# Two attention layers: scores from two fp16 parts in the array's row halves, in two-bank slots

## The chip, the cores and the metric

The kernel runs on one core of one Trainium2 chip. The metric is the device time of one execution in microseconds (us); lower is better. Engines are named as in the profile: PE (TensorE matmuls; PEld its weight loads), DVE (VectorE), ACT (ScalarE), POOL (GpSimd) and SP (SyncE, which here issues DMAs).

## The reference

A stack of four attention layers and four expert layers on x of 8 batches x 512 tokens x 256 features, fp32. The change touches the third layer ("rope") and the seventh ("latent"). Both compute, cut to what matters:

```python
q, k, v = heads(...)                      # 16 heads of 16 features each
q = q * cos + rotate_half(q) * sin        # rotary embedding, the same for k
scores = einsum('bqhd,bkhd->bhqk', q, k) * DH ** -0.5
attn = softmax(scores, axis=-1)           # 512 x 512 for each of 8 batches x 16 heads
out = einsum('bhqk,bkhd->bqhd', attn, v)
x = x + out.reshape(b, l, d) @ Wo         # latent adds a bias; its q is x itself
```

In rope q, k and v are projections of the normalised x. In latent q is the normalised x and k and v come through 128-wide latents, whose two matrices are folded into one before. The layer "decay" before rope has the same shape and keeps the old code.

## The kernel before

Everything is written out by hand for each engine: each has one list of instructions in program order, and semaphores tie the lists together. The layers run one after the other. `mha_layer` builds decay, rope and latent.

**The scores.** A score must be accurate to fp32, and the fast matmul takes bf16. So each rotated q and k is split into three bf16 parts. Of the products of parts six are kept; with 16 features a head that makes 96 rows of contraction. The rows stand in `QS` and `KS` in SBUF, written through DRAM (`write_parts`, L1435; `load_group`, L1448). Softmax needs the row maximum before the exponential. So the scores are computed twice: `max_scores` (L1553) with queries on the partitions, for DVE's maximum over 512 keys (`maxima`, L1819), and `exp_scores` (L1566) with keys on the partitions, for ACT's exponential (L1733), where three more rows (96 to 98) subtract the maximum, itself in three bf16 parts. `split_maxima` (L1839 to L1846) makes these parts, PE turns them (`mT`, L1526), ACT copies them and one DMA writes them into `QS` (L1456).

**The loop.** A batch has 64 steps, one for each of 16 heads x 4 key tiles. In a step PE issues one exp score matmul and one max score matmul of 512 columns, ACT one exponential and DVE one maximum of 128x512. The maxima run 13 to 28 steps ahead. Max scores have three PSUM banks (`psA`) and exp scores two (`psB`), apart from each other. After every fourth step PE multiplies the four probabilities tiles by the values (`value_sums`, L1597: fp32, four heads in four column quarters of the array, two instructions each). The table `USES` puts the rest of PE's work, called uses, into given steps: transposes of the normalised x (`xT`), the projections (`k`, `q`, `v`), the turned outputs (`OT`, `aT`) and the output projection (`Wo`). They share two PSUM banks (`psM`) in turn. ACT empties most of them; DVE normalises the heads from OT (L1853, L1855) and adds Wo to x, with the next layer's statistics (L1868 to L1876).

**The preparation of the next batch.** DVE normalises x (L1774, L1779), shuffles for the rotation (L1805) and multiplies with the cosines (L1793). POOL multiplies with the sines (L1381), adds (L1383), makes part one (L1392) and the two differences (L1396, L1402); ACT makes part two (L1694). Per batch these are four such chains (k and q, each in two halves of 8 heads). SP then writes the parts to DRAM and loads them back. `QS` and `KS` hold one batch, in four groups of four heads.

**The lead-in.** The first batch's chains run on DVE and ACT alone. DVE also adds the expert layer's results of batches 4 to 7 in between (L407, L410, L413). No exponential starts before the first group's maxima are in `QS`.

## Time and profile before

| what | value |
|---|---|
| time, median of 3 runs | 2992.68 us (2987.15 to 2997.36) |
| profiled execution, first to last instruction | 2991.6 us |
| PE / DVE / ACT / POOL busy | 83% / 68% / 54% / 28% |
| mean granted PE clock | 0.915 |
| rope, first to last exponential | 959.6 to 1485.3 us |
| latent, first to last exponential | 2199.5 to 2704.9 us |

The profiled execution's own time is given only as its span, 2991.6 us, 1.1 us below the median of the runs. The shares are averages over layers with different limits, so the two layers are read in windows of their own. A duration of a PE row holds the time until its result is out. The issue of matmuls that follow each other is read from the difference of their starts.

### The profile page before, as it was taken

How to read it: one execution, taken by the hardware profiler on the slowest of the kernel's cores; microseconds unless marked ns; L12 is line 12 of the kernel's file. 1: busy time of each engine (PE TensorE's matmuls, PEld its weight loads, DVE VectorE, ACT ScalarE, POOL GpSimd, SP SyncE). 2: the span in 40 equal slices, each digit the busy share in tenths (PEclk: the TensorE clock that was granted, in tenths of full speed). 3: DMA queues.
4: the chain of work that ended last, by engine and by line, in shares of the span. 5: the costliest groups of instructions: out<-in, count | busy, mean ns of one | idle time of the engine just before them, and what ended most of it. 6: DMA issues, size and time to landing. Idle time of an engine off the chain costs nothing. (4 is left out here: it accounts for less than half of the span.)

```text
span 2991.6 us, 42513 instructions
## 1 busy us (share of the span) xinstructions
PE 2494.0 (83%) x13800; PEld 1260.0 (42%) x13800; DVE 2037.1 (68%) x5246; ACT 1603.7 (54%) x3058; POOL 848.9 (28%) x777
## 2 busy tenths in 40 slices
PE   4899999997575999999857687399789999995598
PEld 2344444443452333333345455266423333333365
DVE  5788888884638788888553444677488888874343
ACT  2477776776423766666652433255347677673122
POOL 0333222220232433322023300445233334302211
PEclk7799999999787999999978899599879999997799
DMA  7565655651164333333026200456343222313232
GB/s 242 179 187 177 181 179 170 179 171 49 56 195 138 96 96 96 101 103 96 13 90 187 66 1 36 175 190 230 124 139 103 90 92 86 116 56 132 96 132 84
DMA packets 217234, 368.47 MB, mean 123 GB/s; under 512 B 21801, under 2 KB 173100, under 8 KB 212280
## 3 DMA queue, kind: packets, MB, share of 16 engines
q1 hardware_dynamic: 201480, 316.35, 33.2%
...
## 5 line engine op out<-in xcount | busy, mean ns | idle before, releaser
L1816 DVE CUSTOM_DVE_ANT_0 decay_junk<-decay_scores_q,decay_corr 128x512 bf16<-128x512 f32 x512 | 338.4, 685 | 111.4 <-PE decay_scores_q L1553 109.6
L1733 ACT ACTIVATE decay_probs<-decay_scores_k 128x512 f32<-128x512 f32 x512 | 294.5, 597 | 188.8 <-PE decay_scores_k L1572 155.1
L1819 DVE TENSOR_REDUCE rope_mx<-rope_scores_q 128x1 f32<-128x512 f32 x512 | 334.0, 685 | 89.9 <-PE rope_scores_q L1553 89.6
L1733 ACT ACTIVATE rope_probs<-rope_scores_k 128x512 f32<-128x512 f32 x512 | 294.6, 600 | 166.3 <-PE rope_scores_k L1566 165.0
L1819 DVE TENSOR_REDUCE latent_mx<-latent_scores_q 128x1 f32<-128x512 f32 x512 | 330.4, 684 | 70.2 <-PE latent_scores_q L1553 69.8
L1733 ACT ACTIVATE latent_probs<-latent_scores_k 128x512 f32<-128x512 f32 x512 | 294.9, 600 | 151.6 <-PE latent_scores_k L1566 149.8
L1553 PE MATMUL decay_scores_q<-decay_KS,decay_QS 96*128 96x512 bf16 x512 | 204.6, 400 | 36.7 <-DVE decay_mx L1816 23.3
L1553 PE MATMUL latent_scores_q<-latent_KS,latent_QS 96*128 96x512 bf16 x512 | 201.3, 395 | 22.7 <-DMA latent_QS<-latent_parts_dram 13.4
L1553 PE MATMUL rope_scores_q<-rope_KS,rope_QS 96*128 96x512 bf16 x512 | 200.8, 394 | 21.5 <-DVE rope_mx L1819 12.8
L1566 PE MATMUL latent_scores_k<-latent_QS,latent_KS 99*128 99x512 bf16 x512 | 197.3, 387 | 6.0 <-ACT latent_probs L1733 2.8
L1566 PE MATMUL rope_scores_k<-rope_QS,rope_KS 99*128 99x512 bf16 x512 | 196.7, 386 | 4.5 <-ACT rope_probs L1733 2.7
L1569 PE MATMUL decay_scores_k<-decay_QS,decay_KS 99*128 99x384 bf16 (+3 forms) x512 | 156.6, 307 | 15.0 <-DMA decay_QS<-decay_mT 7.2
L1597 PE MATMUL decay_out_heads<-decay_probs,decay_Vaug 128*32 128x512 f32 x1024 | 139.0, 615 | 0.8 <-DVE decay_probs L1828 0.8
L1597 PE MATMUL rope_out_heads<-rope_probs,rope_Vaug 128*32 128x512 f32 x1024 | 136.4, 605 | 0.7 <-ACT rope_probs L1733 0.7
L1597 PE MATMUL latent_out_heads<-latent_probs,latent_Vaug 128*32 128x512 f32 x1024 | 136.4, 605 | 0.7 <-ACT latent_probs L1733 0.7
L208 PE MATMUL experts_logits_results<-experts_we,experts_xT 128*128 x384 | 114.2, 426 | 14.4 <-ACT experts_xT L262 9.7
L1566 PEld LDWEIGHTS latent_scores_k<-latent_QS,latent_KS 99*128 99x128 bf16 x512 | 49.1, 97 | 182.6 <-ACT latent_probs L1733 138.3
L1566 PEld LDWEIGHTS rope_scores_k<-rope_QS,rope_KS 99*128 99x128 bf16 x512 | 49.0, 96 | 181.8 <-ACT rope_probs L1733 149.2
L1569 PEld LDWEIGHTS decay_scores_k<-decay_QS,decay_KS 99*128 99x128 bf16 x512 | 49.4, 97 | 174.9 <-issue 86.0
L1381 POOL TENSOR_TENSOR rope_sh<-rope_sh,rope_tab 128x512 f32<-128x512 f32 x28 | 35.5, 1268 | 304.3 <-DVE rope_fc L1793 304.3
L348 DVE TENSOR_TENSOR experts_y<-experts_logits_results,experts_be 128x256 f32<-128x256 f32 x96 | 39.6, 424 | 104.8 <-PE experts_logits_results L208 72.6
L765 ACT ACTIVATE experts4x_hT<-experts4x_inner 128x512 f16<-128x512 f32 x64 | 38.2, 597 | 125.6 <-PE experts4x_inner L669 125.6
...
## 6 DMA issues: line engine op xcount, KB each, us to landing
decay_KS<-decay_parts_dram SPq DMA_DIRECT2D x64, 384.0 KB
decay_QS<-decay_parts_dram SPq DMA_DIRECT2D x64, 384.0 KB
decay_parts_dram<-decay_parts SPq DMA_DIRECT2D x56, 384.0 KB, 3.1
...
```

The source lines that it names most:

```text
L208: last = pe.matmul(psL[:, n % 2, 0:D], xT[:, n % 2, c, :], we[:, c, bass.ds(at, D)], start=(c == 0), stop=(c == 1))
L348: dve.tensor_tensor(y[:, n % RING, :], psL[:, n % 2, 0:D], be[:, bass.ds(at, D)], ALU.add).then_inc(y_taken, 1)
L765: act.activation(hT[:, 0, f, :], psH[:, (n * FC + f) % 3, :], ACT.Relu).then_inc(h_high, 1)
L1381: eng.tensor_tensor(sh[:, j % 2, :], sh[:, j % 2, :], tab[:, 1, :], ALU.mult).then_inc(sin_done, 1)
L1553: pe.matmul(psA[:, A_BANK[k], :], QS[0:96, 0, c, hh, qt * P:(qt + 1) * P], KS[0:96, NV - 1, c, hh, :], start=True, stop=True).then_inc(a_r ...
L1566: last = pe.matmul(psB[:, s % 2, :], KS[:, 0, c, hh, keys], QS[:, 0, c, hh, :], start=True, stop=True)
L1569: last = pe.matmul(psB[:, s % 2, 0:end], KS[:, 1, c, hh, keys], QS[:, 0, c, hh, 0:end], start=True, stop=True)
L1597: last = pe.matmul(psO[32 * h:32 * h + 32, :], Vaug[:, b % 2, kt, 4 * grp + h, :], probs[:, (b * 16 + kk) % PSLOTS, h, :], start=(kt == 0) ...
L1733: act.activation(probs[:, (b * 16 + kk) % PSLOTS, h, :], psB[:, s % 2, :], ACT.Exp, scale=scale).then_inc(exp_done, 1)
L1816: dve.tensor_tensor_reduce(junk[:, a % 2, :], psA[:, A_BANK[k], :], corr[:, qt, :], 1.0, -3.0e38, ALU.mult, ALU.max, mx[:, grp % 2, qt, h: ...
L1819: dve.tensor_reduce(mx[:, grp % 2, qt, h:h + 1], psA[:, A_BANK[k], :], AX.X, ALU.max).then_inc(a_done, 1)
```

## The change

Rope and latent are built by a new function, `mha_pairs`. Decay keeps `mha_layer`.

- Each rotated q and k is split into two fp16 parts. Three of their products are kept: 48 rows of contraction for a head. To stay in fp16's range, k and q are scaled by powers of two that are found once in the lead-in from the largest weight (`scales`); in latent the tables hold a factor of 32.
- Two heads are handled in a step. One stands in partitions 0 to 47, the other in 64 to 111, so each matmul uses one half of the array's rows. The two results go into the two banks of one slot. Two more rows in each half (48 and 49) subtract the maximum in two fp16 parts.
- A batch has 32 steps. In each, PE issues two exp score matmuls and two max score matmuls, ACT one exponential and DVE one maximum, each of 128x1024.
- PSUM: max and exp scores share one ring of three two-bank slots, taken in turn. The uses share one bank in place of two.
- The maxima run 16 steps ahead. Their parts are turned by DVE (32x32 blocks), written to DRAM and read back by SP into `QS`.
- `QS` and `KS` hold two batches, each in two halves of 8 heads.
- POOL takes over the cosine products (L1793 before) and the normalising of x after the first two batches (L1774, L1779 before). The middle part on ACT and one difference go.
- `value_sums` is as before, after every second step. `USES` is a new table, with a use in every even step (rope) or all but two of these (latent).

The core of the diff:

```diff
+def mha_pairs(nc, g, ins, project_q, biased, results):
...
+    STEPS, NM = 32, 8
...
+    USES = [(0, "k0"), (2, "q0"), (4, "OT3"), (6, "aT1"), (8, "Wo0"), (10, "Wo1"), (12, "OT0"), (14, "k1"), (16, "q1"),
+            (18, "v0"), (20, "OT1"), (22, "aT0"), (24, "v1"), (26, "xT0"), (28, "OT2"), (30, "xT1")]
+    if not project_q:
+        USES = [(u, name) for u, name in USES if name[0] != "q"]
...
+    ROTATE_AT = [2, 4, 16, 18]
+    NORMALISE_AT, PV_AT = 18, 1
...
+    scores = [("top", n) for n in range(16)]
+    for n in range(NB * STEPS):
+        scores += [("exp", n)] + ([("top", n + 16)] if n + 16 < NB * STEPS else [])
...
+        psS = ctx.enter_context(nc.psum_tensor(f"{g['layer']}_scores", [P, 3, 2, S], F32))
+        psO = ctx.enter_context(nc.psum_tensor(f"{g['layer']}_out_heads", [P, S], F32))
+        psM = ctx.enter_context(nc.psum_tensor(f"{g['layer']}_work", [P, S], F32))
...
+        parts = sb("parts", [P, 4, 2, S], F16)
+        QS, KS = (sb(n, [P, 2, 2, 4, S], F16) for n in ("QS", "KS"))
+        probs = sb("probs", [P, 2, 4, S], F32)
...
+        def wait_slot(eng, kind, n):
+
+            at = place[kind, n] - 3
+            if at >= 0:
+                before, k = scores[at]
+                eng.wait_ge(exp_done if before == "exp" else a_done, k + 1)
...
+            def write_parts(nb, j):
+
+                o, c = CHAINS[j]
+                sp.wait_ge(low_done, nb * 4 + j + 1)
+                rows = rows_of(nb, o, c).rearrange("(j d) (h t) -> (d h) j t", d=16, h=8)
+                for first, n, i in ((0, 2, 0), (2, 1, 1)) if o == "k" else ((1, 2, 0), (0, 1, 1)):
+                    sp.dma_start(rows[:, first:first + n, :], parts[:, j, i:i + 1, :].to_broadcast([P, n, S])).then_inc(
+                        parts_written[j], 16)
+
+            def load_half(nb, c):
+
+                for j in (2 * c, 2 * c + 1):
+                    sp.wait_ge(parts_written[j], 32 * (nb + 1))
+                if nb >= 2:
+                    sp.wait_ge(b_ready, (nb - 2) * STEPS + 16 * (c + 1))
+                for o, to in (("k", KS), ("q", QS)):
+                    for y in range(2):
+                        sp.dma_start(to[64 * y:64 * y + 48, nb % 2, c, :, :].rearrange("r l s -> r (l s)"),
+                                     rows_of(nb, o, c)[:, 4 * y * S:(4 * y + 4) * S]).then_inc(half_loaded[c], 16)
...
+                             mpT[:, n % 2, :]).then_inc(rows_written[n % 2], 16)
+
...
+                sp.wait_ge(rows_written[n % 2], 16 * (n // 2 + 1))
+                for y in range(2):
+                    sp.dma_start(QS[64 * y + 48:64 * y + 50, nb % 2, c, at:at + 2, :],
+                                 rowscr[n][4 * y:4 * y + 4, :]).then_inc(rows_loaded[grp], 16)
...
+            def max_scores(n):
...
+                wait_slot(pe, "top", n)
+                qt, hp = divmod(a, 2)
+                c, l = heads_of(grp, hp)
+                for y in range(2):
+                    rows = slice(64 * y, 64 * y + 48)
+                    last = pe.matmul(psS[:, slot_of("top", n), y, :], QS[rows, nb % 2, c, l, qt * P:(qt + 1) * P],
+                                     KS[rows, nb % 2, c, l, :], start=True, stop=True)
+                last.then_inc(a_ready, 1)
...
+            def exp_scores(b, u):
...
+                wait_slot(pe, "exp", b * STEPS + u)
+                c, l = heads_of(grp, hp)
+                for y in range(2):
+                    rows = slice(64 * y, 64 * y + 50)
+                    last = pe.matmul(psS[:, slot_of("exp", b * STEPS + u), y, :],
+                                     KS[rows, b % 2, c, l, kt * P:(kt + 1) * P], QS[rows, b % 2, c, l, :], start=True, stop=True)
+                last.then_inc(b_ready, 1)
...
+                pe.wait_ge(exp_done, b * STEPS + 2 * kk + 2)
...
+            for b in range(NB):
+                for u in range(STEPS):
+                    exp_scores(b, u)
+                    if top_of(b, u) is not None:
+                        max_scores(top_of(b, u))
+                    if u % 2 == PV_AT:
+                        if u > PV_AT:
+                            value_sums(b, u // 2 - 1)
+                        elif b:
+                            value_sums(b - 1, 15)
+                    for name, nb in uses_at(b, u):
+                        work(name, nb)
...
+                    if u % 2 == 0 and kk >= 2:
+                        act.wait_ge(pv_done, kk - 1)
+                    act.wait_ge(b_ready, n + 1)
+                    act.activation(probs[:, kk % 2, 2 * (u % 2):2 * (u % 2) + 2, :], psS[:, slot_of("exp", n), :, :], ACT.Exp,
+                                   scale=escale[:, 0:1]).then_inc(exp_done, 1)
+                    if u % 8 == PV_AT + 1:
+                        if grp:
+                            take_heads(b, grp - 1)
+                        elif b:
+                            take_heads(b - 1, 3)
+                    for name, nb in uses_at(b, u - 1) if u else uses_at(b - 1, STEPS - 1):
+                        if name[:2] not in TURNED_BY_DVE:
+                            take(name, nb)
...
+            def rotate(nb, j):
+
+                n = nb * 4 + j
+                of, src = turned_from(j)
+                emptied(dve, of, nb)
+                if n >= 2:
+                    dve.wait_ge(sum_done, n - 1)
+                dve.stream_shuffle(sh[:, j % 2, :], src, [i ^ 8 for i in range(32)]).then_inc(rot_done, 1)
...
+            def maxima(n):
...
+                dve.wait_ge(a_ready, n + 1)
...
+                dve.tensor_reduce(mx[:, grp % 2, :, hp, qt], psS[:, slot_of("top", n), :, :], AX.X, ALU.max).then_inc(a_done, 1)
...
+                flat = mx[:, grp % 2, :, :, :].rearrange("p y l t -> p y (l t)")
+                dve.tensor_scalar(mp[:, 0, :, 0, :], flat, -1.0 / LEVEL, None, ALU.mult).then_inc(split_done, 1)
+                dve.wait_ge(split_done, 2 * n + 1)
+                dve.scalar_tensor_tensor(mp[:, 0, :, 1, :], flat, -1.0 / LEVEL, mp[:, 0, :, 0, :], ALU.mult,
+                                         ALU.subtract).then_inc(split_done, 1)
...
+                dve.transpose(mpT[:, n % 2, :], mp[:, 0, :, :, :].rearrange("p y s r -> p (y s r)")).then_inc(rows_turned, 1)
...
+            for b in range(NB):
+                for u in range(STEPS):
+                    if top_of(b, u) is not None:
+                        maxima(top_of(b, u))
+                    if u % 8 == 0 and b * 4 + u // 8 + 1 < NB * 4:
+                        split_maxima(*divmod(b * 4 + u // 8 + 1, 4))
+                    for name, nb in uses_at(b, u - 1) if u else uses_at(b - 1, STEPS - 1):
+                        if name[:2] in TURNED_BY_DVE:
+                            (normalise_heads if name[:2] == "OT" else add_out)(nb, int(name[-1]))
+                    if b + 1 < NB and u in ROTATE_AT:
+                        rotate(b + 1, ROTATE_AT.index(u))
...
+            for b in range(NB):
+                for u in range(STEPS):
+                    if b + 2 < NB and u == NORMALISE_AT:
+                        pool.wait_ge(m_ready, turn["xT1", b + 1] + 1)
+                        for t in range(4):
+                            normalise(pool, b + 2, t)
+                        if biased:
+                            add_bias(b + 2)
+                    if b + 1 < NB and u in ROTATE_AT:
+                        j = ROTATE_AT.index(u)
+                        cosines(pool, b + 1, j)
+                        rotary_sum(pool, b + 1, j)
+                        high_part(pool, b + 1, j)
+                        low_part(pool, b + 1, j)
+
+
 def single_head_layer(nc, g, ins, results):
...
-                "rope", mha_layer, rope, False, HD ** -0.5, True, False, (), results))
+                "rope", mha_pairs, rope, True, False, results))
...
-                "latent", mha_layer, latent, False, HD ** -0.5, False, True, (), results))
+                "latent", mha_pairs, latent, False, True, results))
```

TensorE's order, a stretch of a middle batch of rope, before:

```order
L1566 MATMUL rope_scores_k<-rope_QS,rope_KS 128x512
L1553 MATMUL rope_scores_q<-rope_KS,rope_QS 128x512
L1597 MATMUL rope_out_heads<-rope_probs,rope_Vaug 32x512 x4
L1566 MATMUL rope_scores_k<-rope_QS,rope_KS 128x512
L1553 MATMUL rope_scores_q<-rope_KS,rope_QS 128x512
L1566 MATMUL rope_scores_k<-rope_QS,rope_KS 128x512
L1553 MATMUL rope_scores_q<-rope_KS,rope_QS 128x512
L1526 MATMUL rope_work<-identb,rope_mp 12x128 x4
L1566 MATMUL rope_scores_k<-rope_QS,rope_KS 128x512
L1553 MATMUL rope_scores_q<-rope_KS,rope_QS 128x512
L1539 MATMUL rope_work<-rope_wo,rope_attnT 128x256 x2
```

The same engine in a middle batch of the changed rope (L2305 exp scores, L2292 max scores, L2318 values, L2278 and L2261 uses):

```order
L2305 MATMUL rope_scores<-rope_QS,rope_KS 128x512 x2
L2292 MATMUL rope_scores<-rope_KS,rope_QS 128x512 x2
L2318 MATMUL rope_out_heads<-rope_probs,rope_Vaug 32x512 x4
L2305 MATMUL rope_scores<-rope_QS,rope_KS 128x512 x2
L2292 MATMUL rope_scores<-rope_KS,rope_QS 128x512 x2
L2278 MATMUL rope_work<-rope_wv,rope_xnT 128x256 x4
L2305 MATMUL rope_scores<-rope_QS,rope_KS 128x512 x2
L2292 MATMUL rope_scores<-rope_KS,rope_QS 128x512 x2
L2318 MATMUL rope_out_heads<-rope_probs,rope_Vaug 32x512 x4
L2305 MATMUL rope_scores<-rope_QS,rope_KS 128x512 x2
L2292 MATMUL rope_scores<-rope_KS,rope_QS 128x512 x2
L2261 MATMUL rope_work<-ident_sb,rope_xn 128x128 x4
```

Between two values there are now two pairs of each kind where there were four single matmuls of each. The uses come as a whole after a pair of pairs, where a large one was cut in halves before. The turning of the maxima (L1526) is gone.

SP's order for one middle batch of rope, before, from the row maxima of group 1 to those of the next batch's group 0:

```order
L1456 DMA rope_QS<-rope_mT 3x4x512
L1435 DMA rope_parts_dram<-rope_parts 128x3x512
L1435 DMA rope_parts_dram<-rope_parts 128x2x512
L1435 DMA rope_parts_dram<-rope_parts 128x512
L1435 DMA rope_parts_dram<-rope_parts 128x3x512
L1435 DMA rope_parts_dram<-rope_parts 128x2x512
L1435 DMA rope_parts_dram<-rope_parts 128x512
L1456 DMA rope_QS<-rope_mT 3x4x512
L1448 DMA rope_KS<-rope_parts_dram 96x2048
L1448 DMA rope_QS<-rope_parts_dram 96x2048
```

And the changed one, from the row maxima of group 3 (L2210 writes them to DRAM, L2219 reads them) to those of the next batch's group 0, with the parts of chains 2 and 3 (L2192) and the load of the second half (L2203):

```order
L2210 DMA rope_tops_dram<-rope_mpT 4x32x32
L2219 DMA rope_QS<-rope_tops_dram 2x1024 x2
L2192 DMA rope_parts_dram<-rope_parts 128x2x512
L2192 DMA rope_parts_dram<-rope_parts 128x512
L2192 DMA rope_parts_dram<-rope_parts 128x2x512
L2192 DMA rope_parts_dram<-rope_parts 128x512
L2210 DMA rope_tops_dram<-rope_mpT 4x32x32
L2203 DMA rope_KS<-rope_parts_dram 48x2048 x2
L2203 DMA rope_QS<-rope_parts_dram 48x2048 x2
L2219 DMA rope_QS<-rope_tops_dram 2x1024 x2
```

A row maximum takes two transfers where it took one. The next batch's first maxima are read after the load of its second half, which waits for the parts of chains 2 and 3.

VectorE's order in a middle batch of the changed rope, around the two additions to x (L2503 maxima, L2537 to L2545 the addition and its statistics, L2524 and L2526 the normalising of heads):

```order
L2503 TENSOR_REDUCE rope_mx<-rope_scores 128x2
L2537 TENSOR_TENSOR X<-X,rope_work 128x2x256
L2540 BN_STATS rope_st<-X 128x6 x2
L2543 BN_AGGR rope_mv<-rope_st 128x2 x2
L2545 COPY X<-rope_mv 128x2x2
L2503 TENSOR_REDUCE rope_mx<-rope_scores 128x2 x2
L2537 TENSOR_TENSOR X<-X,rope_work 128x2x256
L2540 BN_STATS rope_st<-X 128x6 x2
L2543 BN_AGGR rope_mv<-rope_st 128x2 x2
L2545 COPY X<-rope_mv 128x2x2
L2503 TENSOR_REDUCE rope_mx<-rope_scores 128x2 x2
L2524 RECIPROCAL rope_rec<-rope_work 128x16
```

One maximum now covers what two did, so the two additions stand two maxima apart; before it was also two, of half the size.

## Rows read from the trace of the kernel before

**Rows 1.** Busy time of rope's lead-in, rope's middle and latent's middle:
```profile
core 0: us, PE busy (x) PEld busy (x) DVE busy (x) ACT busy (x) POOL busy (x), PEclk, DMA share, GB/s
902.40:959.60 57.20, 32.03 (x74) 11.80 (x75) 49.07 (x120) 15.42 (x32) 16.33 (x16) 0.65 0.56 172
...
1052.00:1446.00 394.00, 386.29 (x2043) 149.19 (x2042) 321.27 (x671) 268.63 (x497) 123.29 (x110) 1.00 0.30 94
...
2265.00:2651.00 386.00, 376.65 (x2042) 145.90 (x2041) 329.90 (x709) 270.73 (x499) 145.84 (x125) 1.00 0.31 98
```

**Rows 2.** Rope's and latent's exponentials, all of the run:
```profile
L1733 ACT ACTIVATE rope_probs<-rope_scores_k x512: 582/597/631, 959.6 to 1485.3; 128x512 f32<-128x512 f32 x171
...
L1733 ACT ACTIVATE latent_probs<-latent_scores_k x512: 582/597/629, 2199.5 to 2704.9; 128x512 f32<-128x512 f32 x171
```

**Rows 3.** Groups by line (busy, mean ns, idle before), middles of rope, latent:
```profile
L1566 PE MATMUL rope_scores_k<-rope_QS,rope_KS 99*128 99x512 bf16 x376 | 144.6, 385 | 1.5 <-ACT rope_probs L1733 0.4
...
L1819 DVE TENSOR_REDUCE rope_mx<-rope_scores_q 128x1 f32<-128x512 f32 x378 | 247.7, 685 | 68.3 <-PE rope_scores_q L1553 68.2
...
L1566 PE MATMUL latent_scores_k<-latent_QS,latent_KS 99*128 99x512 bf16 x381 | 146.6, 385 | 1.6
```

**Rows 4.** TensorE in order of time, one stretch of rope's middle:
```profile
1200.70 0.63 PE L1531 MATMUL rope_work<-ident_sb,rope_Osb 128*128 128x128 f32 x4
1201.16 0.38 PE L1566 MATMUL rope_scores_k<-rope_QS,rope_KS 99*128 99x512 bf16 x1
1201.38 0.38 PE L1553 MATMUL rope_scores_q<-rope_KS,rope_QS 96*128 96x512 bf16 x1
1201.69 1.06 PE L1597 MATMUL rope_out_heads<-rope_probs,rope_Vaug 128*32 128x512 f32 x8
1202.69 0.39 PE L1566 MATMUL rope_scores_k<-rope_QS,rope_KS 99*128 99x512 bf16 x1
...
1204.43 1.03 PE L1539 MATMUL rope_work<-rope_wo,rope_attnT 128*128 128x256 f32 x4
1205.30 0.38 PE L1566 MATMUL rope_scores_k<-rope_QS,rope_KS 99*128 99x512 bf16 x1
```

**Rows 5.** Groups by shape in the causal layer:
```profile
L2164 ACT ACTIVATE causal_probs<-causal_masked,causal_nm 128x512 f32<-128x512 f32 x8 | 5.8, 722 | 25.1 <-DVE causal_nm L2242 25.1
...
L2239 DVE CUSTOM_DVE_ANT_0 causal_masked<-causal_scores,causal_mask 128x512 f32<-128x512 f32 x8 | 5.5, 692 | 22.1 <-PE causal_scores L2071 22.1
...
L2164 ACT ACTIVATE causal_probs<-causal_masked,causal_nm 128x128 f32<-128x128 f32 x8 | 3.2, 402 | 2.7 <-DVE causal_nm L2242 2.7
...
L2239 DVE CUSTOM_DVE_ANT_0 causal_masked<-causal_scores,causal_mask 128x128 f32<-128x128 f32 x8 | 2.3, 292 | 37.1 <-PE causal_scores L2071 21.7 <-DMA rope_KS<-rope_onesrow 15.3
```

**Rows 6.** VectorE groups beside the maxima, rope's middle; latent's normalising:
```profile
L1793 DVE TENSOR_TENSOR rope_fc<-rope_f,rope_tab 128x512 f32<-128x512 f32 x21 | 15.6, 742 | 0.0
L1805 DVE STREAM_SHUFFLE rope_sh<-rope_f 128x512 f32<-128x512 f32 x21 | 15.5, 736 | 0.0
...
L1774 DVE TENSOR_SCALAR rope_xn<-X 128x256 f32<-128x256 f32 x20 | 8.1, 405 | 0.0
...
L1779 DVE TENSOR_SCALAR latent_xn<-X 128x128 f32<-128x128 f32 x40 | 12.9, 389 | 0.0
```

**Rows 7.** VectorE in order of time, end of rope:
```profile
1493.22 0.69 DVE L1868 TENSOR_TENSOR X<-X,rope_work 128x512 f32<-128x512 f32 x1 [4.03 <-PE rope_work L1539]
...
1495.09 0.68 DVE L1868 TENSOR_TENSOR X<-X,rope_work 128x512 f32<-128x512 f32 x1
```

**Rows 8.** GpSimd groups, rope's middle:
```profile
L1383 POOL TENSOR_TENSOR rope_fc<-rope_fc,rope_sh 128x512 f32<-128x512 f32 x22 | 28.1, 1277 | 1.7
...
L1392 POOL CAST rope_parts<-rope_fc 128x512 bf16<-128x512 f32 x22 | 15.5, 704 | 1.4
```

**Rows 9.** DMA issues (KB each, median us to landing):
```profile
rope_parts_dram<-rope_parts SPq DMA_DIRECT2D x32, 384.0 KB, 2.7
rope_KS<-rope_parts_dram SPq DMA_DIRECT2D x32, 384.0 KB, 4.1
```

424 lines of the change are left out of this document (418 added, 6 removed).

## The prediction

> **What bounds the kernel now.** I read the busy windows first, to see which engine is full in the two changed layers, then the groups by line, then TensorE in order of time. In rope's middle, 394 us, PE is busy 386 at a granted clock of 1.00, DVE 321 and ACT 269; latent's middle looks alike [rows 1]. Those 394 us hold 376 exponentials, so a batch of 64 takes 67.1 us; latent's 381 in 386 us give 64.8 [rows 1, 3]. Exp scores waited 1.5 us in all and the maxima 68 us, nearly all for PE [rows 3]. So PE sets the pace and DVE is next.
>
> PE's time is in the starts, not the durations. A score matmul issues every 0.22 us (1201.16 to 1201.38). A values group costs 0.31 from the score before it, and 1.00 to the score after it: 1.31, or 1.09 more than a score alone. A turned OT costs 0.46 and half a Wo 0.87 [rows 4]; a k or q projection streams as many columns as a whole Wo (1.73). Before, a rope batch needs 128 x 0.22 = 28.2, 16 x 1.09 = 17.4, eight large uses 13.8, eight small ones 3.9, and four turned maxima 1.6 (at 0.4 each, less than an OT): 64.9 of the 67.1. In latent, without q, 61.5 of the 64.8.
>
> **The scores on PE.** If the two row halves run side by side, a pair of 512 columns costs the 0.22 of one: 64 x 0.22 = 14.1, so 14.1 go. No row here has row halves. The nearest are the values: eight instructions of 512 columns in four column quarters issue in 1.00 us, where eight in a row at a score's pace would need 1.76 [rows 4]. The array does run quarters side by side. The bounds are 0.22 and 0.44 a pair; I take 0.22.
>
> A score after values waits longer than a score after a score: entering costs 0.09 more, and leaving about 0.15 (1.00 against the 0.85 of a half Wo's columns) [rows 4]. The switch to and from a use costs nothing visible today. The changed scores stand in a layout of the array that neither values nor uses have, so I charge 0.24 for each of 16 uses: 3.9 us; none and 0.48 are the bounds. The four turned maxima (1.6) go. PE then needs 14.1 + 17.4 + 13.8 + 3.9 + 3.9 = 53.1 us for a rope batch and 49.2 for latent.
>
> The Trainium skill, "TensorEngine Tiling (Array Packing)", Tiling Modes, says that a change of tiling mode drains the engine. That speaks against this change, which has more of them; the trace agrees at the values, with the 0.09 and 0.15 above. With no drain charged at the uses the PE sum would be 49.2 for rope.
>
> **DVE and ACT.** The slopes come from the causal layer: DVE 692 to 292 ns over 384 columns is 1.04 ns a column, ACT 722 to 402 is 0.83 [rows 5]. A maximum of 1024 then takes 685 + 533 = 1.22 us, 1.18 back to back, so 32 of them 37.9 us where 64 take 42.2 [rows 3]. An exponential takes 0.60 + 0.43 = 1.03: 33 us a batch, with 14 copies of some 0.58 (estimate from the 0.60) 41. ACT stays third.
>
> DVE's other work is (321.3 - 247.7) / 5.87 batches = 12.5 us [rows 1, 3]. The cosine products (four of 0.74) and rope's normalising (four of 0.41) leave it [rows 6]; with one operation less in the split and a transpose more, about 9 of work and 11 to 12 with the waits between dependent operations remain. DVE needs some 49 us, close to PE's 53.
>
> **What the shared slots make of it.** PE's and DVE's sums aren't reached, because buffering gets thinner. An exp pair may be written only when the maximum of two steps before is done, a max pair only when the exponential of the step before is done. So PE can run about one step ahead of DVE, where it had separate rings before. I count by pairs of steps, each the larger of two sums:
> - PE: an odd step is 0.44 + 1.09 = 1.53, an even step with a large use 0.44 + 1.97 = 2.41, with a small one about 1.17. So 3.94 or 2.70 (2.8 with the waits for the shared bank).
> - DVE: 2.36 for two maxima, and beside them a shuffle 0.62, a split 0.6, a normalising of heads 0.7, or an addition to x with its statistics, 1.87 [rows 7].
> - Rope: six pairs with a large use at 3.94; the two with Wo are DVE's, 4.9 and 4.3; the pair at step 4 3.7; three with heads 3.1; four 2.8. The sum is 23.6 + 9.2 + 3.7 + 9.3 + 11.2 = 57. Waits of uses for their one bank (a k projection behind the normalising of heads, twice) add about 2: 59.
> - Latent: two of the large pairs lose q and become 3.1 and 3.8: 56 to 58.
>
> **The preparation on POOL, and SP.** The chain is now cosine, sine, sum, high, low: 4 x 1.27 + 0.70 = 5.8 us [rows 8]. Its start is a shuffle in steps 2, 4, 16 and 18. POOL also normalises between chains 2 and 3. POOL has no row for this; its sum takes 1.27 where DVE's product takes 0.74, so I scale by 1.8 [rows 6, 8]: rope 4 x 0.73 = 2.9. Latent 8 x 0.70 = 5.6, and 2.4 for the bias. Bounds are DVE's own times (1.6 and 3.1) and twice my figures. In rope step 16 is at about 32 us: shuffle at 34.5, chain 2 to 40.5, normalising to 43.4, chain 3 to 49.2, parts out at 53.3 (1.1 to issue, 2.7 to 3 to land), loads issued to 55, landed at 58.5 (half the size of a 4.1 us load today) [rows 9]. It is needed at 59: just in time. In latent the same gives 61 to 61.5 against 58, so the next batch's first scores wait some 3 us and a batch takes 61.5. That cost has no cover: exp and max scores of step 0 both stand behind it. The row maxima's way through DRAM (about 0.7 + 2.5 + 1.4 + 2.5 = 7 us) lies inside eight steps of 1.8 us, and the scratch traffic falls to half.
>
> **The sum.** Rope: six middle batches 6 x (67.1 - 59) = 49. First and last took 526 - 6 x 67.1 = 124 together [rows 2]. The new first lacks four uses (54), and the new last has maxima only in its first 16 steps and then runs at ACT's pace (46): with a cold start 104, so 20. Rope 69. Latent: 6 x (64.8 - 61.5) = 20, and 117 against 102 for first and last: 15; 35. The lead-ins get longer: the power-of-two scales (some ten small operations across PE and DVE), the second batch normalised and turned ahead of the first maximum, and the first row maxima through DRAM. In rope's lead-in PE has only 0.65 of its clock and is busy 32 of 57 us, so nothing there is PE's [rows 1]. I count 5 for rope and 4 for latent, between 0 (hidden behind the additions of results) and 10 each. Gain 69 + 35 - 9 = 95. From the span of 2991.6, that is 2897; the median of the runs is 1.1 higher, so I say 2897.
>
> **Rivals.**
> - *Free flow.* Uses don't pay for a switch, waits overlap better, and both layers run at 55 and 57: rope 6 x 12.1 + 24 = 97, latent 6 x 7.8 + 20 = 67, less 9: 2837. For it: PE before reached 97% of its sum. Against: slots are coarser and DVE at 49 of 55 would be nearly full.
> - *Late halves.* POOL's normalising or the DMAs are slower than I scale, and each batch ends in a wait: rope 62, latent 66. Rope 31 + 16, latent -7 + 8, less 12: 2956. For it: the time to the deadline in rope is under 1 us. Against: SP and POOL are otherwise free.
> - *Row halves in turn (the slower side).* If a pair costs 0.44, PE needs 67.2 in rope and 63.3 in latent, and with the loss to thin slots 70.5 and 68.5. Middles lose 20 and 22, first and last give back 14, the lead-ins cost 12: 3032. The point where it decides: a pair of about 0.33, where PE's 60 passes DVE's pair sums. For it: each half needs its own weights, and a weight load of 128 columns hides behind 0.22 us today, but two must. Against: the four quarters of the values. The Trainium skill, "TensorE: Matmul & The Clock Gate", Part 3, gives 3.07 times for four row tiles; no run here shows it. By that a pair would cost about 0.25 and the rope batch 2 us more, on PE only.
> - The clock is no case of its own. The middles run at 1.00, which is 2.4 GHz, and the lead-in, where PE waits for long, at a mean of 0.65 [rows 1]. Waits of a microsecond between PE's 53 of 59 us should not bring it down; if a wait of several did, each batch of the late halves would lose a microsecond more, and that case would end at 2970.
>
> **Chances.** Forecast 0.56, free flow 0.14, late halves 0.15, halves in turn 0.15. Within 0.3% (9 us, about what a measurement of this kernel can tell from no change) lies only a thin part between the last two, 0.04. Faster by more 0.84, slower by more 0.12. The forecast's own range is 2865 to 2935; the range of 8 in 10 takes in free flow and late halves, 2835 to 2970, and leaves out halves in turn.
>
> **What would show it.** Rope's exponentials to be 256 of about 1.03 us, maxima 256 of 1.22; the two matmuls of a pair to start within a few tens of ns and the next pair 0.22 later; an issue of 0.3 between scores and a use; middle batches of 59 and 61.5 us; DVE busy about 0.83 of them; in latent a wait of some 3 us for a DMA into KS or QS each 32 steps. I am wrong if the second matmul of a pair starts 0.2 us after the first, if POOL's normalising is over 1 us each, or if DVE and PE wait for each other all along with neither over 0.8.

## The result, and the profile after

| | before | changed kernel |
|---|---|---|
| time, median | 2993.65 us (2987.15 to 2997.36, 4 runs) | 2944.56 us (2938.81 to 2948.00, 4 runs) |
| profiled execution | 2991.6 us | 2937.1 us |
| rope, first to last exponential | 525.7 us | 465.6 us |
| latent, first to last exponential | 505.4 us | 495.5 us |
| middle batches, rope / latent | 68.2 / 65.1 us | 59.5 to 61.5 / 65.3 to 65.9 us |

The ratio is 0.983, interval 0.982 to 0.985: 49 us less, where 95 were forecast. Between the two profiled executions it is 54.5 us, since the changed kernel's is the fastest of its four. Rope gave 60 of the 69 forecast, latent 10 of 35. The lead-ins cost 6.1 and 6.6 us more than before, where 5 and 4 were charged. Together that is 57 us; the 3 between it and the 54.5 lie in stretches that the change leaves alone. These move by several us from execution to execution: rope's start lies anywhere from 896.7 to 904.6 us in the runs below. A middle batch is the time from its first exponential to the next batch's; before, the six rope ones had a first-to-first time of 68.2, a little over the 67.1 that [rows 1, 3] gave by count.

First the busy time by windows, which answers to [rows 1]: rope's lead-in, rope's middle, latent's batches from the second on, and 6 us behind one of latent's borders.

```profile
core 0: us, PE busy (x) PEld busy (x) DVE busy (x) ACT busy (x) POOL busy (x), PEclk, DMA share, GB/s
911.00:968.20 57.20, 30.99 (x76) 12.05 (x76) 44.36 (x98) 15.24 (x31) 11.79 (x12) 0.62 0.30 82
1020.00:1378.00 358.00, 326.65 (x2002) 113.52 (x1998) 292.62 (x431) 250.32 (x274) 156.70 (x140) 1.00 0.20 55
2216.00:2650.00 434.00, 354.13 (x2232) 120.51 (x2228) 321.69 (x477) 282.82 (x300) 177.10 (x165) 0.95 0.17 45
...
2281.00:2287.00 6.00, 6.00 (x26) 1.90 (x26) 2.92 (x5) 2.73 (x3) 0.00 (x0) 0.74 0.02 3
```

In rope PE is busy 0.91 and DVE 0.82. In latent PE has 0.82 and DVE 0.74: both wait for something else. The exponentials and the groups by line of rope's middle, which answer to [rows 2, 3, 6, 8]:

```profile
L2426 ACT ACTIVATE rope_probs<-rope_scores,rope_escale x256: 1106/1114/1172, 968.2 to 1433.8; 128x1024 f32<-128x1024 f32 x128
```
```profile
L2426 ACT ACTIVATE latent_probs<-latent_scores,latent_escale x256: 1107/1115/1172, 2152.9 to 2648.4; 128x1024 f32<-128x1024 f32 x128
```
```profile
L2503 DVE TENSOR_REDUCE rope_mx<-rope_scores 128x2 f32<-128x1024 f32 x191 | 233.2, 1224 | 61.5 <-PE rope_scores L2292 60.8
...
L2305 PE MATMUL rope_scores<-rope_QS,rope_KS 50*128 50x512 f16 x384 | 74.8, 386 | 6.6 <-DMA rope_QS<-rope_tops_dram 5.4 <-DVE rope_mx L2503 1.3
...
L2148 POOL TENSOR_TENSOR rope_parts<-rope_fc,rope_parts 128x512 f16<-128x512 f32 x24 | 27.8, 1157 | 1.9
L2160 POOL TENSOR_SCALAR rope_xn<-X 128x256 f32<-128x256 f32 x20 | 24.2, 1219 | 0.0
```

A maximum took 1.224 us (forecast 1.22), an exponential 1.115 (1.03), one of POOL's normalisings in rope 1.22 (0.73). Next, PE in order of time across a border of two rope batches, in answer to [rows 4]; in a score row x2 is one pair, one matmul in each row half.

```profile
1202.11 0.39 PE L2305 MATMUL rope_scores<-rope_QS,rope_KS 50*128 50x512 f16 x2
1202.34 0.38 PE L2292 MATMUL rope_scores<-rope_KS,rope_QS 48*128 48x512 f16 x2
...
1206.21 0.39 PE L2305 MATMUL rope_scores<-rope_QS,rope_KS 50*128 50x512 f16 x2 [0.89 <-DMA rope_QS<-rope_tops_dram]
1206.44 0.38 PE L2292 MATMUL rope_scores<-rope_KS,rope_QS 48*128 48x512 f16 x2
1206.75 1.98 PE L2265 MATMUL rope_work<-rope_xnT,rope_wk 128*128 128x512 f32 x4
1208.66 0.39 PE L2305 MATMUL rope_scores<-rope_QS,rope_KS 50*128 50x512 f16 x2
```

The pair takes the 0.39 of one matmul and the next pair starts 0.23 later: the row halves run side by side. From scores into a use it takes 0.31 (1206.44 to 1206.75), and at rope's border the row maxima come 0.89 us late (2.2 at the worst border): "just in time", as forecast. Latent's border is another matter. First what PE waited for in latent, then PE, SP and POOL at one border.

```profile
PE latent_scores L2305 <- DMA latent_QS<-latent_tops_dram: 37.4, 6, 6.6
PE latent_scores L2292 <- ACT latent_probs L2426: 19.3, 23, 1.1
PE latent_work L2272 <- DVE latent_attn L2526: 7.7, 14, 0.7
PE latent_work L2265 <- DVE latent_attn L2526: 7.3, 7, 1.1
```
```profile
2273.79 1.06 PE L2318 MATMUL latent_out_heads<-latent_probs,latent_Vaug 128*32 128x512 f32 x8
2280.99 0.61 PE L2305 MATMUL latent_scores<-latent_QS,latent_KS 50*128 50x512 f16 x2 [6.14 <-DMA latent_QS<-latent_tops_dram]
2281.40 0.63 PE L2292 MATMUL latent_scores<-latent_KS,latent_QS 48*128 48x512 f16 x2
2281.96 3.06 PE L2265 MATMUL latent_work<-latent_xnT,latent_wk 128*128 128x512 f32 x4
```
```profile
2273.02 0.52 SPq L2210 DMA_DIRECT2D latent_tops_dram<-latent_mpT  x1
2274.67 0.79 SPq L2203 DMA_DIRECT2D latent_KS<-latent_parts_dram  x2
2275.51 0.89 SPq L2203 DMA_DIRECT2D latent_QS<-latent_parts_dram  x2
2276.44 0.57 SPq L2219 DMA_DIRECT2D latent_QS<-latent_tops_dram  x2
```
```profile
2251.51 1.27 POOL L2127 TENSOR_TENSOR latent_fc<-latent_f,latent_tab 128x512 f32<-128x512 f32 x1 [15.83 <-DVE latent_sh L2495]
...
2257.32 6.51 POOL L2165 TENSOR_SCALAR latent_xn<-X 128x128 f32<-128x128 f32 x8
2263.91 2.37 POOL L2603 TENSOR_TENSOR X<-X,latent_xb 128x1024 f32<-128x1024 f32 x1
2266.24 1.27 POOL L2127 TENSOR_TENSOR latent_fc<-latent_xnT,latent_tab 128x512 f32<-128x512 f32 x1
...
2270.91 1.16 POOL L2148 TENSOR_TENSOR latent_parts<-latent_fc,latent_parts 128x512 f16<-128x512 f32 x1
```

Read backwards: PE stood 6.14 us for the row maxima's DMA, which stood in SP's queue behind the loads of the second half, and these behind chain 3, which stood on POOL behind 8.9 us of normalising and bias. Ahead of it POOL had been idle for 15.83 us. And the wait has a second price: the granted clock behind the border is 0.74 (a mix of 2.4 and 1.2 GHz; PE had been idle for 6 us), so the k projection takes 3.06 us and not 1.98.

### The profile page after: what moved, and what is told of

Same layout as the page of the kernel before. It is cut to its first block and busy times, and to the rows that moved or that the text cites. A ratio compares the mean times of both kernels' runs of the same rounds, so it can differ in the third digit from the quotient of the medians.

```text
span 2937.1 us, 40653 instructions
## 1 busy us (share of the span) xinstructions
PE 2314.2 (79%) x13550; PEld 1158.7 (39%) x13550; DVE 1943.5 (66%) x4549; ACT 1537.0 (52%) x2426; POOL 912.0 (31%) x851
## 5 line engine op out<-in xcount | busy, mean ns | idle before, releaser
L2503 DVE TENSOR_REDUCE latent_mx<-latent_scores 128x2 f32<-128x1024 f32 x256 | 310.1, 1222 | 111.0 <-PE latent_scores L2292 110.7
L2426 ACT ACTIVATE latent_probs<-latent_scores,latent_escale 128x1024 f32<-128x1024 f32 x256 | 282.3, 1116 | 189.8 <-PE latent_scores L2305 189.0
L2426 ACT ACTIVATE rope_probs<-rope_scores,rope_escale 128x1024 f32<-128x1024 f32 x256 | 283.5, 1116 | 152.4 <-PE rope_scores L2305 151.6
L2503 DVE TENSOR_REDUCE rope_mx<-rope_scores 128x2 f32<-128x1024 f32 x256 | 311.1, 1223 | 78.7 <-PE rope_scores L2292 77.6
L2318 PE MATMUL latent_out_heads<-latent_probs,latent_Vaug 128*32 128x512 f32 x1024 | 137.2, 608 | 6.7 <-ACT latent_Osb L2417 4.1
L2318 PE MATMUL rope_out_heads<-rope_probs,rope_Vaug 128*32 128x512 f32 x1024 | 137.2, 608 | 6.0 <-ACT rope_Osb L2417 4.1
L2305 PE MATMUL latent_scores<-latent_QS,latent_KS 50*128 50x512 f16 x512 | 101.3, 395 | 40.5 <-DMA latent_QS<-latent_tops_dram 37.4
L2292 PE MATMUL latent_scores<-latent_KS,latent_QS 48*128 48x512 f16 x512 | 103.5, 402 | 31.4 <-ACT latent_probs L2426 19.3
L2292 PE MATMUL rope_scores<-rope_KS,rope_QS 48*128 48x512 f16 x512 | 101.4, 394 | 18.0 <-DVE rope_mx L2503 7.9
L348 DVE TENSOR_TENSOR experts_y<-experts_logits_results,experts_be 128x256 f32<-128x256 f32 x96 | 39.7, 423 | 104.4 <-PE experts_logits_results L208 60.1
L58 POOL DMA_INDIRECT dispatched<-experts_XN,experts_slot x64 | 62.5, 976 | 144.5 <-DVE experts_slot L337 100.2
L2305 PE MATMUL rope_scores<-rope_QS,rope_KS 50*128 50x512 f16 x512 | 99.7, 389 | 8.4 <-DMA rope_QS<-rope_tops_dram 5.4
L1572 PE MATMUL decay_scores_k<-decay_QS,decay_KS 99*128 99x256 bf16 (+2 forms) x384 | 104.8, 273 | 0.0
```

Of the source, the lines that this page charges most:

```text
L1572: last = pe.matmul(psB[:, s % 2, end:S], KS[:, 0, c, hh, keys], QS[:, 1, c, hh, end:S], start=True, stop=True)
L2292: last = pe.matmul(psS[:, slot_of("top", n), y, :], QS[rows, nb % 2, c, l, qt * P:(qt + 1) * P], KS[rows, nb % 2, c, l, :], start=True, st ...
L2305: last = pe.matmul(psS[:, slot_of("exp", b * STEPS + u), y, :], KS[rows, b % 2, c, l, kt * P:(kt + 1) * P], QS[rows, b % 2, c, l, :], star ...
L2318: last = pe.matmul(psO[32 * h:32 * h + 32, :], Vaug[:, b % 2, kt, 4 * grp + h, :], probs[:, kk % 2, h, :], start=(kt == 0), stop=(kt == 3))
L2426: act.activation(probs[:, kk % 2, 2 * (u % 2):2 * (u % 2) + 2, :], psS[:, slot_of("exp", n), :, :], ACT.Exp, scale=escale[:, 0:1]).then_in ...
L2503: dve.tensor_reduce(mx[:, grp % 2, :, hp, qt], psS[:, slot_of("top", n), :, :], AX.X, ALU.max).then_inc(a_done, 1)
```

## The experiments

Every run gives this table: the mean time, over batches 1 to 5 of the layer, from one exponential's start to the next but one's, for pairs of steps (worked out from ScalarE's rows in order of time). "0+1" are steps 0 and 1. A large pair of steps holds one of the projections or half a Wo, a small one a transpose or no use. The names are those of the runs below; POOL normalises at step 18 in the first six rows and at step 6 in the rest.

```
rope, us          0+1   2+3  10+11 14+15 20+21 30+31  batch  | latent batch
changed kernel   3.99  4.10  4.45  5.20  2.98  4.13   60.1   | 65.6
heads first      4.53  4.08  4.00  3.99  2.98  4.62   58.9   | 64.4
same rows        4.84  4.85  4.87  5.48  3.51  3.56   68.0   | 69.3
uses with values 4.89  5.10  5.06  5.02  3.57  3.57   68.6   | 67.6
whole rows       4.55  4.54  4.77  5.48  3.41  3.46   65.3   | 67.6
rows ahead       5.13  4.07  4.45  5.20  2.98  3.14   60.2   | 64.6
normalise early  3.99  4.09  4.45  5.20  2.98  3.14   59.2   | 57.3
early + heads    3.99  4.09  4.00  3.99  2.98  2.98   56.9   | 55.5
constant scale   3.99  4.00  4.45  5.21  2.89  3.15   58.6   | 56.7
max of one head  3.99  4.09  4.00  4.01  2.98  2.98   56.3   | 54.4
values first     3.99  4.09  4.10  4.08  3.04  3.04   58.8   | 56.9
```

**1. Normalise early.**
```diff
-    NORMALISE_AT, PV_AT = 18, 1
+    NORMALISE_AT, PV_AT = 6, 1
```


> One number is changed: GpSimd normalises batch b + 2 (and adds latent's bias) at step 6 of 32, in the some 16 us in which it is idle, not at step 18 between chains 2 and 3. Theory (late halves): latent's five full batches of 65.3 to 65.9 us end in a wait of up to 6.6 us for the row maxima's DMA because the second half's scores came late; with 8.9 us of POOL work out of the way they fall to the 58.7 us of the one batch that has nothing to normalise. Latent gains 6 x 6.8 = 40, less what the 1.4 us of lead of rope's borders gives or takes: 2905 us, between 2898 and 2912. Rival (coupling of PE and DVE by the slots): the wait at the border is only where the loss is seen, and another wait takes its place; the batches stay above 63 us and the time above 2930. Rope: its border waits are only 0.9 us, so it moves by under 5 us in all.

Measured: 2880.35 us (2877.81 to 2890.16), ratio to before 0.963 (0.960 to 0.966). That is 18 us below the range that I had given. Latent's batches are 57.2 to 57.5 us, its first 56.1 (63.4 in the changed kernel), and the wait for the row maxima is gone; the other waits are as they were:

```profile
PE latent_scores L2292 <- ACT latent_probs L2426: 18.8, 22, 1.1
PE latent_work L2272 <- DVE latent_attn L2526: 7.7, 14, 0.7
PE latent_work L2265 <- DVE latent_attn L2526: 7.3, 7, 1.1
```

The late halves are shown, and no wait took their place. The range was missed in latent: I had reckoned with 40 us from latent and under 5 from rope; latent gave 50.4 (445.1 us from first to last exponential), since the clock's fall goes too (step 0 takes 2.39 us, not 4.13), and rope 7.4: its border also waited, up to 2.2 us at a time. The two layers make 57.8 of the 64.2 us. Of the rest, 3.2 is the difference between the medians and the profiled executions, and in these rope's start came 7.2 us earlier (897.4 for 904.6), the stretch from rope's last exponential to latent's first took 6.1 more (725.2 for 719.1) and the end behind latent 1.9 less, none of which the edit touches. So the time per layer is a finer measure here than the whole.

**2. Heads first.** In VectorE's step the `for` over uses stands ahead of `maxima(top_of(b, u))` and the split.
```diff
+                    for name, nb in uses_at(b, u - 1) if u else uses_at(b - 1, STEPS - 1):
+                        ...
                     if top_of(b, u) is not None:
                         maxima(top_of(b, u))
```


> In each step VectorE does the normalising of heads or the addition to x, which frees PE's one work bank, ahead of the step's maximum and not behind it. In rope PE waited about 26 us in uses for VectorE to free that bank (7.7 before the q projections, 7.3 before v, 5.4 before two of the turnings of xn, 2.7 and 2.5 before others), in latent about as much. Theory A (the bank's waits are real cost on PE): half to all of it comes back, rope 60 to 58 us a batch, some 12 to 20 us a layer: 2910 to 2925. Theory B (VectorE is the co-bound: the maximum comes later by just as much, and its slot is late for PE): no change within 5 us, 2944. Worse than 2950 would say that slots matter more than the bank.

Measured: 2923.02 us (2922.17 to 2925.49), ratio 0.977 (0.974 to 0.979): theory A, in part. Rope lost 8.2 us from first to last exponential and latent 5.9, where I had 12 to 20 for each; that the whole, 21.5 us less, lies in theory A's range is in part the luck of the executions. Pair 14+15 falls from 5.20 to 3.99 and 10+11 from 4.45 to 4.00, but rope's border grows: steps 30, 31 and 0 together from 6.53 to 7.46. What PE wins in the middle it waits for at the border, where the row maxima's DMA is still late; run 5 tests that.

**3. Same rows.**
```diff
-                    rows = slice(64 * y, 64 * y + 48)
+                    rows = slice(0, 48)
```
and in `exp_scores` `slice(0, 50)`.

> Both matmuls of every score pair take their operands from partitions 0 up, so nothing runs side by side in the array's row halves; the second head's scores are left out (the first's stand in for them) and the rest is unchanged. This measures what the row halves are worth. Theory: a pair costs 0.44 in place of 0.22 us, 64 pairs a batch add 14.1 us to PE's about 53, and a rope batch goes from 60 to between 67 and 72 us, a latent one (49 + 14 = 63 of PE) to 67 to 72 too: 8 x 7 to 12 plus 8 x 2 to 7, so 3020 to 3090 us, slower than before the change. Rival (PE is not the bound any more, VectorE and the slots are): under 3 us a batch, 2950 to 2990.

Measured: 3083.49 us (3058.73 to 3100.83), ratio 1.032 (1.028 to 1.036). PE in order of time:

```profile
1205.19 0.60 PE L2305 MATMUL rope_scores<-rope_QS,rope_KS 50*128 50x512 f16 x2
1205.63 0.59 PE L2292 MATMUL rope_scores<-rope_KS,rope_QS 48*128 48x512 f16 x2
1206.16 1.98 PE L2265 MATMUL rope_work<-rope_xnT,rope_wq 128*128 128x512 f32 x4
1208.07 0.60 PE L2305 MATMUL rope_scores<-rope_QS,rope_KS 50*128 50x512 f16 x2
```

A pair now takes 0.44 (1205.19 to 1205.63), twice the 0.23, and a large pair of steps 4.84 for 3.99: 0.85, which is four times the 0.21 of a pair. So in these steps PE is the bound, and the row halves are worth 8 us a rope batch: without them a rope batch takes 68.0, as before the change (68.2). The whole says less. Its four times spread over 42 us, and in the profiled execution, the fastest, latent's first batch took 81.6 us, with PE busy for 78 of them at a granted clock of 0.73, where the next took 70.1; why is open.

**4. Uses with the values.**
```diff
+    USES = [(u + 1, name) for u, name in USES]
```


> Every use (projection or transposes in the work bank) moves one step later, from the even steps to the odd ones, right behind the values group of that step: the array then switches from scores to values and uses and back once in two steps, not twice. PE's sum falls by 16 x about 0.24 to 0.28 us a batch = 3.9 to 4.5. Theory A (PE's own sum sets the pace): batches fall by 2 to 4 us, 2885 to 2915. Theory B (the slots couple PE to VectorE step by step): an odd step is now 0.44 + 1.09 + 1.97 = 3.5 us on PE, and VectorE's 1.2 us and ScalarE's 1.1 us a step can not run on through it because only three slots are filled ahead; the gain of the switches is eaten and batches get longer, by 1 to 4 us: 2955 to 3005.

Measured: 3015.31 us (3007.60 to 3016.82), ratio 1.007 (1.005 to 1.010), beyond theory B's range. A rope batch takes 68.6 us. The wait that grew, in rope:

```profile
PE rope_scores L2293 <- ACT rope_probs L2427: 91.2, 111, 1.1
```

A max pair may be written when the exponential of the step before is done. With values in odd and a use in even steps PE has something to do meanwhile; with both in the odd step the even one holds score pairs alone, and PE then waits for its exponential ahead of the odd step's max pair, 0.8 us on average. Three slots are one step of slack: the order must spread PE's other work evenly.

**5. Early and heads first.** Edits 1 and 2 together.

> Both single changes at once: POOL normalises at step 6, and VectorE frees the work bank ahead of the maximum. Heads first alone took 2 us out of rope's steps 0 to 30, but its step 31 grew from 2.58 to 3.53 us: the border ended in the same wait for late row maxima. Theory (the two causes are separate, and the border hid part of the second): rope 59.1 to about 57.0 us a batch, latent 57.3 to about 55.2, so 2880 less 8 x 2.1 x 2 = 34: 2847 us, 2840 to 2858. Rival (VectorE is the co-bound, what PE wins at the bank it loses at the slots once the border is free): batches of 58.5 and 57, 2870 to 2880.

Measured: 2856.88 us (2851.08 to 2865.34), ratio 0.954 (0.952 to 0.956). Rope's batches are 56.9 (57.0 expected), latent's 55.5 (55.2); the causes are separate. The whole came out at the range's end: against run 1 rope lost 13.6 us and latent only 6.0, since latent's first and last batch got longer (58.1 and 47.6 us for 56.1 and 45.4). This is the fastest version that leaves nothing out, 88 us below the changed kernel.

**6. Constant scale.** On edit 1:
```diff
-                                   scale=escale[:, 0:1]).then_inc(exp_done, 1)
+                                   scale=0.001).then_inc(exp_done, 1)
```


> POOL at step 6 as before, and the exponential takes a constant as its scale in place of a column of 128 values (a fixed 0.001, so the scale that the weights ask for is left out). The exponential of 1024 took 1.115 us where I had estimated 1.03 from slopes with a constant scale. Theory: the column is the difference, so 1.02 to 1.04 here; and ScalarE is not the bound, only the four or five steps without a use (1.09 and 1.89 us) follow it: 0 to 0.8 us a batch, 2868 to 2881 us. Rival 1: the slope over two banks is steeper, and the exponential stays at 1.11. Rival 2: each step waits for the exponential of the step before, so 32 x 0.09 = 2.8 us a batch, 2835 us.

Measured: 2870.87 us (2866.88 to 2873.38), ratio 0.958 (0.956 to 0.960).

```profile
L2426 ACT ACTIVATE rope_probs<-rope_scores x256: 1018/1023/1110, 966.6 to 1421.0; 128x1024 f32<-128x1024 f32 x128
```

1.023 us, my 1.03: the column as a scale costs 0.09 us. The Trainium skill, "ScalarE: Activation LUTs", section What ACT_TABLE_LOAD costs, gives 186 ns + 0.833 ns a column with immediates and about 93 ns more for each column operand. Estimates by it are 1.04 and 1.13 us; both runs agree within 2%. A pair with a small use falls from 2.98 to 2.89, by one exponential's 0.09, large ones hardly: a batch gains 0.6.

**7. Max of one head.** On edit 1, `psS[:, slot, 0:1, :]` in `maxima`, with `mx` cleared once.

> POOL at step 6, and each row maximum is taken over the first head of its slot alone, 512 columns and not 1024 (the second head's maxima are left out and stand at 0): VectorE's operation falls from 1.22 to 0.66 or 0.69 us, 17 us a batch less. This measures how far VectorE bounds the layers. Theory: PE's sum with its switches sets the pace, and VectorE only sets the steps where a use waits behind a maximum (step 14 of 3.61 us, step 10 of 2.85, four with heads): 1.5 to 3 us a batch, 2832 to 2856 us. Rival (VectorE is a co-bound through the slots all along): 5 us a batch or more, down to PE's 53 and 49: below 2800.

Measured: 2833.33 us (2829.54 to 2837.25), ratio 0.946 (0.944 to 0.948).

```profile
L2503 DVE TENSOR_REDUCE rope_mx<-rope_scores 128x1 f32<-128x512 f32 x193 | 132.8, 691 | 138.8 <-PE rope_scores L2292 137.3
```

VectorE's work falls by 17 us a batch and the batch by 2.9 (rope) and 2.9 (latent): the theory. It goes where it was said to go, 10+11 and 14+15, and in small pairs with heads; large pairs and 20+21 don't move. VectorE is no co-bound all along, only its order in a few steps is, and run 5 had 2.3 of the 2.9 in rope by order alone.

**8. Whole rows.** As run 3, with `rows = slice(0, 128)` at both places.

> As the run with both matmuls of a pair on one row half, but every score matmul now contracts over all 128 partitions (so both heads' rows are summed, with the unused rows at 0, and the exponential's scale is 2 to the 20th smaller; the scores of single heads are left out). The scores then have the array layout of the projections and transposes, and only the values group differs. POOL stays at step 18, so only rope's steady batches compare: 68.0 us there. Theory (a use in another layout costs a switch of 0.24 to 0.28 us): steps with a large use fall from 2.83 to 2.55 to 2.6 us, eight of them, the small ones are bound by the exponential's way (1.5 us) and stay: rope 68.0 to 65.8 to 66.4 us. Rival 1 (the switch is part of any change from scores to a use): no change, 68.0. Rival 2 (loading twice as many rows of weights costs more than 0.22 a matmul): above 70 us.

Measured: 3021.60 us (3018.55 to 3032.34), ratio 1.010 (1.008 to 1.012).

```profile
1201.91 0.60 PE L2305 MATMUL rope_scores<-rope_QS,rope_KS 128*128 128x512 f16 x2
1202.35 0.59 PE L2292 MATMUL rope_scores<-rope_KS,rope_QS 128*128 128x512 f16 x2
1202.79 1.88 PE L2265 MATMUL rope_work<-rope_xnT,rope_wq 128*128 128x512 f32 x4
1204.50 0.59 PE L2305 MATMUL rope_scores<-rope_QS,rope_KS 128*128 128x512 f16 x2
```

A score pair still takes 0.44, with 128 rows of weights or with 48. Into the q projection it takes 0.44 and out of it 1.71; in run 3 0.53 and 1.91. The switch costs 0.09 + 0.20 = 0.29 a use, and large pairs show it: 4.84 to 4.55. The batch falls by 2.7 us to 65.3, a little more than expected, because small pairs gain 0.1 too. The Trainium skill, "TensorEngine Tiling (Array Packing)", Tiling Modes, says that a change of mode drains the engine; this agrees, with 0.29 us as its price here.

**9. Rows ahead of parts.** In SP's queue:
```diff
                     write_parts(b + 1, 2)
-                    write_parts(b + 1, 3)
                     write_rows(b + 1, 0)
-                    load_half(b + 1, 1)
                     load_rows(b + 1, 0)
+                    write_parts(b + 1, 3)
+                    load_half(b + 1, 1)
```


> POOL normalises at step 18 as in the changed kernel; only SP's queue is in another order: the first row maxima of the next batch are written and loaded ahead of the parts of chain 3, not behind them and behind the loads of the second half. They are ready at step 24, and in latent they waited in the queue: written at 2273.02, loaded from 2276.44, needed some 8 us before 2280.99. Theory 1 (queue order): the row maxima were late only because SP stood at chain 3's parts, and step 0's exp pair now comes in time, but its max pair needs the second half, whose loads were issued from 2274.67 and land some 3.5 to 4 us later: the border keeps some 5 of its 8.3 us (the clock's fall after the wait, 1.7 of them, included), latent goes from 65.6 to 62 to 64 us a batch, 2944 less 6 x 2.5 = 2930, 2918 to 2938. Theory 2 (the row maxima alone were late): the border's wait is gone, latent 58 us a batch, 2900. Theory 3 (the halves decide alone): 65.6 as it was, 2944.

Measured: 2944.34 us (2938.45 to 2952.85), ratio 0.984 (0.982 to 0.987): no change, theory 3. Latent's batches are 64.1 to 65.3. PE at a border, SP at the same one, and PE's wait in all:

```profile
2277.05 0.39 PE L2305 MATMUL latent_scores<-latent_QS,latent_KS 50*128 50x512 f16 x2
2282.82 0.60 PE L2292 MATMUL latent_scores<-latent_KS,latent_QS 48*128 48x512 f16 x2 [5.37 <-DMA latent_QS<-latent_parts_dram]
```
```profile
2276.99 0.78 SPq L2203 DMA_DIRECT2D latent_KS<-latent_parts_dram  x2
2277.81 0.89 SPq L2203 DMA_DIRECT2D latent_QS<-latent_parts_dram  x2
```
```profile
PE latent_scores L2292 <- DMA latent_QS<-latent_parts_dram: 32.4, 6, 6.2
```

The exp pair of step 0 starts on time and the max pair behind it stands for the second half. The name in the changed kernel's row of waits, the row maxima, was only the last in a queue. From the first load's issue to the max pair it took 5.8 us, where I had put 3.5 to 4, and so I expected a gain (2918 to 2938).

**10. Values first.** On run 5, `value_sums` stands ahead of `max_scores` in a step.

> On top of POOL at step 6 and VectorE's heads first, PE's order in odd steps is exp pair, values group, max pair, and not exp, max, values. It tests the picture of the slots. Where a small use stands, a pair of steps takes 2.98 us for PE's 2.7, because the max pair of the odd step waits for the exponential of the step before (1.89 of 1.60). Theory A (that wait alone costs): the values cover it, five odd steps in rope and six in latent fall from 1.89 to 1.60: 1.5 us a batch, 2857 less 24 = 2833. Theory B (a max pair that comes 1.09 us later makes its maximum late for the exp pair that reuses the slot two steps on): what is won in the odd step is lost in the next, even one; pairs with a small use go to 3.1 us, large ones stay: 2850 to 2885.

Measured: 2883.79 us (2878.61 to 2887.49), ratio 0.964 (0.962 to 0.965): 27 us slower than run 5, theory B. Small pairs take 3.04 for 2.98, and those where VectorE has a use besides more (12+13 went from 3.60 to 4.36). The wait is for the maximum, as said:

```profile
PE rope_scores L2305 <- DVE rope_mx L2503: 32.4, 64, 1.4
```

## Why the prediction was right in its mechanism and half in its size

Direction, mechanism and range (2835 to 2970) held; the time came out at 2944.6 and not 2897, beyond the forecast's own range of 2865 to 2935 and nearer to the late halves (2956). What happened is the forecast in rope and the late-halves rival in latent.

| step | predicted | measured | |
|---|---|---|---|
| a pair of 512 columns | 0.22 us | 0.22 to 0.23; 0.44 on one row half | right |
| switch per use | 0.24 | 0.29 | right, a fifth too low |
| maximum, exponential | 1.22, 1.03 | 1.224, 1.115 | the scale's column was missed |
| rope, pair with a large use | 3.94 | 3.99 to 4.10 | right |
| rope, middle batch | 59 | 60.1 (59.2 in run 1) | right, in part by luck |
| first rope batch, first and last together | 54 without a cold start, 104 with it | 59.0, 105.9 | 2 too low |
| rope before: middle batch, first and last together | 67.1, 124 | 68.2, 116.6 | misread |
| normalising on POOL, rope / latent | 2.9 / 5.6 + 2.4 | 4.9 / 6.5 + 2.4 | too low |
| latent, free pace | 58 | 57.3 (run 1) | right |
| latent, border | 3.5 us | 8.3 us | the step that failed |
| lead-ins | 5 + 4 | 6.1 + 6.6 | low |

**Latent's border** was mis-sized, and it is the step that failed: 3 to 3.5 us over the free pace where 8.3 came (65.6 less 57.3), at six borders. By its parts, from a batch's first exp pair at 2215.66: chain 2 started at 35.9 us, where my 61 to 61.5 us imply about 32.5. Of those 3.4, 1.7 is step 0, run at the fallen clock (4.13 for 2.39), 1 is the first sixteen steps themselves (30.9 at free pace for my 30), and the rest the shuffle, which VectorE began only behind a maximum and a split. POOL's two works took 8.9 for 8.0. From the end of chain 3 (56.4) to the next exp pair (65.3) it was 8.9 us, 9.3 reckoned. So no single duration was badly off. The largest part lies in the form of the sum: I put the late half at the end of a batch that starts at full clock. But each wait lets the clock fall, the fallen clock delays chain 2 by 1.7 us, and the next border is later by that. The prediction names this feedback only for the late halves ("a microsecond more"), whose 66 us a batch came true; I gave them 0.15, and didn't ask what the clock does behind the wait that my own sum already had in latent. One of my signs of being wrong was met, too: a normalising on POOL took over 1 us in rope (1.22). Latent's seventh batch, for which nothing is left to normalise, took 58.7 us without any edit. So latent's six middle batches gave 3 us in place of 20, and its first and last 7 in place of 15, for the first ends in such a wait too (63.4 us, 56.1 in run 1).

**Rope.** A plain large pair came within 0.2 us of its sum. That the whole batch did so too (59.2 in run 1 for 59) is partly luck, since the groups of pairs miss in both directions: the six large ones took 25.5 for 23.6, with 5.20 for 14+15 alone, the four small ones 12.9 for 11.2, but the two with Wo and the one at step 4 only 11.4 for 12.9. The charge of "about 2" for the shared bank closes the sum. Before, with two banks, PE had no wait over 0.15 us for one of them in rope's middle. That VectorE's place in the step could give this back (run 5) the prediction missed.

**First and last batches.** Nine us of rope's shortfall lie here, and most of it in the reading of the kernel before. The six middle batches gave 49.5 us, as forecast (49). But a batch before took 68.2 and not the 67.1 that I had from a count of exponentials in a window, so its first and last together were 116.6 and not 124; they gave 10.7 us where I had 20. In the changed kernel they took 105.9 for my 104. The first alone was 59.0: its missing uses saved 4 us and not 5, and its cold start took 3 (exponentials 0 and 1 lie 5.4 us apart, 2.4 in later batches), of which 1.8 is the first k projection, 3.78 us at a granted clock of 0.50:

```profile
968.71 0.61 PE L2292 MATMUL rope_scores<-rope_KS,rope_QS 48*128 48x512 f16 x2 [0.53 <-DVE rope_mx L2503]
969.25 3.78 PE L2265 MATMUL rope_work<-rope_xnT,rope_wk 128*128 128x512 f32 x4
972.96 0.61 PE L2305 MATMUL rope_scores<-rope_QS,rope_KS 50*128 50x512 f16 x2
```

**Lead-ins,** from the reciprocal of the deviations (904.6, 2095.7; before 902.1, 2148.9) to the first exponential: 63.6 and 57.2 us against 57.5 and 50.6. The first sixteen maxima run at 1.14 us each, two rows of eight in 9.15 and 9.10 us, and the scales' small operations lie from 906.6 to 912.2. What each costs isn't shown.

**The rivals.** Free flow needed batches of 55 and 57: rope doesn't reach its 55 even with a third less work on VectorE (56.3 in run 7); latent does reach its 57 once its border's wait is gone (57.3 in run 1). Row halves in turn was priced at 3032 with batches of 70.5 and 68.5; run 3, the kernel that has it, gave 68.0 and 69.3, and 3083 in all.
